# A mixture-of-experts stage on one core: twelve expert weights fetched ahead in place of nine, four token gathers before the combine weights, and two VectorE blocks cut into pieces

## The reference

```python
logits = xf @ gate_w.T                     # 1024 tokens, 32 experts
w, idx = jax.lax.top_k(logits, 2)
w = jax.nn.softmax(w, axis=-1)
combine = zeros((T, 32)).at[arange(T)[:, None], idx].add(w)
def body(acc, params):
    W, b, c = params                       # W 512 x 512, b 512, c this expert's column of combine
    return (acc + c[:, None] * (xf @ W.T + b), None)
out, _ = jax.lax.scan(body, zeros_like(xf), (expert_w, expert_b, combine.T))
x = x + tanh(g_ffn[1]) * out
```

## Time and profile before

| | us |
|---|---|
| median of 3 runs (lowest, highest) | 904.82 (903.89, 906.77) |
| the profiled execution | 904.44 |
| its span, first to last instruction | 902.6 |
| PE busy in the span | 830.1 |
| DVE busy | 656.1 |
| POOL busy | 424.7 |
| ACT busy | 397.6 |

### The profile page before, as it was taken

The page is one execution under the profiler, slowest core; times in us unless marked ns, Lnnn a source line. Parts: engine busy times, 40 slices in busy tenths (PEclk is TensorE's granted clock), DMA queues, the critical chain, the costliest instruction groups (busy, mean ns, idle before and its releaser), DMA issues. The chain is left out here.

```text
span 902.6 us, 13118 instructions
## 1 busy us (share of the span) xinstructions
PE 830.1 (92%) x4337; PEld 698.7 (77%) x4337; DVE 656.1 (73%) x1300; ACT 397.6 (44%) x1010; POOL 424.7 (47%) x386
## 2 busy tenths in 40 slices
PE   5889999999999999999999999978989897989980
PEld 4778888888888888888888888766877686877860
DVE  3788888867778867778876788774481765999975
ACT  4644244334335324324424334333224535978970
POOL 5489658336347525436634625302010257665730
PEclk9999999999999999999999999999999968999995
DMA  8401102001201101101300210007000846999717
GB/s 330 163 1 52 66 1 102 16 1 47 71 1 58 58 0 46 70 1 46 116 0 0 82 58 1 0 1 298 1 12 1 307 167 209 359 338 327 309 37 280
DMA packets 23641, 91.13 MB, mean 101 GB/s; under 512 B 6576, under 2 KB 7088, under 8 KB 15776
## 3 DMA queue, kind: packets, MB, share of 16 engines
q1 hardware_dynamic: 17440, 81.00, 24.4%
q0 software_dynamic: 6144, 9.46, 3.0%
HBM read 86.23 MB, written 14.68 MB: 112 GB/s over the span
## 5 line engine op out<-in xcount | busy, mean ns | idle before, releaser
L478 ACT ACTIVATE probs<-bank,negmax 128x128 f32<-128x128 f32 x256 | 90.7, 366 | 135.8 <-DVE negmax L605 135.8
L370 POOL TENSOR_TENSOR qT<-straight,turned 128x512 f32<-128x512 f32 x64 | 83.1, 1299 | 141.6 <-DVE turned L594 141.4
L594 DVE TENSOR_TENSOR turned<-bank,sinT 64x512 f32<-64x512 f32 x160 | 110.1, 688 | 2.2
L129 PE MATMUL bank<-wo_hi,oT_hi 128*128 128x512 f32 x256 | 100.5, 392 | 6.2 <-DVE oT_lo L618 6.2
L129 PE MATMUL bank<-xT_hi,wq_hi 128*128 128x512 f32 x256 | 104.4, 408 | 2.0 <-DVE xT_lo L105 2.0
L131 PE MATMUL bank<-xT_hi,wq_lo 128*128 128x512 f32 x256 | 100.2, 391 | 0.0
L131 PE MATMUL bank<-wo_hi,oT_lo 128*128 128x512 f32 x256 | 99.9, 390 | 0.0
L130 PE MATMUL bank<-wo_lo,oT_hi 128*128 128x512 f32 x256 | 99.7, 389 | 0.0
L130 PE MATMUL bank<-xT_lo,wq_hi 128*128 128x512 f32 x256 | 99.6, 389 | 0.0
L485 ACT ACTIVATE pT_hi<-bank 128x512 fp32r<-128x512 f32 x64 | 38.3, 599 | 128.4 <-PE bank L763 128.3
L592 DVE TENSOR_TENSOR straight<-bank,cosT 128x512 f32<-128x512 f32 x80 | 55.3, 691 | 40.5 <-PE bank L131 36.6
(11 more groups left out here) (229 smaller groups left out, 2094.2 us busy)
## 6 DMA issues: line engine op xcount, KB each, us to landing
ring<-in_ew SPq DMA_DIRECT2D x28, 1024.0 KB, 7.6
raw_big<-in_wq SPq DMA_DIRECT2D x8, 1024.0 KB, 4.8
raw_big<-in_wo SPq DMA_DIRECT2D x8, 1024.0 KB, 4.8
early_w<-in_ew SPq DMA_DIRECT2D x8, 1024.0 KB, 7.6
ring<-picked SPq DMA_DIRECT2D x8, 512.0 KB, 7.3
raw_k<-in_wk SPq DMA_DIRECT2D x8, 256.0 KB, 5.1
ctx_raw<-in_ctxT SPq DMA_DIRECT2D x4, 512.0 KB, 6.0
raw_v<-in_wv SPq DMA_DIRECT2D x8, 256.0 KB, 4.9
```

The source lines that it names most:

```text
L129: nc.tensor.matmul(out_, hi, r_hi, start=start, stop=False)
L370: nc.gpsimd.tensor_tensor(dst, straight[:, k, :], turned[:, k, :], ALU.add).then_inc(rope_sum, 1)
L478: ex = nc.scalar.activation(probs[:, u % 2, h, :], bank_scores[u % 2][:, h * S:(h + 1) * S], ACT.Exp, bias=negmax[:, u % UNITS, h:h + 1], ...
L594: last = nc.vector.tensor_tensor(turned[dst, k, :], bank[src, :], sinT[src, tok], ALU.mult)
```

## The change

1. The ring has 11 buffers that are used again, and one more (`at_far`, expert 11) that is used once, so 12 weights are fetched ahead. The two new buffers lie over the upper halves of `xT_hi` and `xT_lo`; turned tokens now use 4 tiles, the lower halves. Expert 11's weight is issued beside experts 0 and 1; experts 9 and 10 are issued with experts 2 to 6, ahead of the `xn_rows` writes. Weights 12 to 22 wait for slot k - 12, later ones for slot k - 11. `at_place` moves from `xT_lo` to the second half of `cT_lo`.
2. POOL issues `take(0)` to `take(3)` ahead of `combine_weights`.
3. COMB is 3 instead of 2: the transposes, bias matmuls and `add_bias` stand in slots 3 to 10 instead of 2 to 9.
4. `far_slots` is cut into five pieces, after slots 3 to 7. `owners` is cut into three, after slots 16 to 18, and its 16 comparisons are one operation of 512 elements. `far_places` waits until expert 11's weight has been split.
5. Semaphores are merged: the loads of context, gate weights, numbers and pair codes share `g_tables` and are all waited for at 64; `r_chosen` is counted in `r_coded`.

```diff
-        RING = 9
-        COMB = 2
+        RING = 11
+        AHEAD = RING + 1
+        TURNED = 4
+        COMB = 3
...
-        at_place = xT_lo[:, 0:2, :].rearrange("p c (j n) -> p (c j) n", n=P)
...
...
-        w_in = [sem(f"w_in{k}") for k in range(RING)]
+                over("xT_hi", "ring9", [P, KC, T])[:, :, T // 2:], over("xT_lo", "ring10", [P, KC, T])[:, :, T // 2:]]
+        w_in = [sem(f"w_in{k}") for k in range(AHEAD)]
...
+        at_far = kept("at_far", [P, NB * TOP, P], F32R)
+        ring.append(over("at_far", "ring11", [P, KC, E])[:, :, :])
...
         def turned_hi(k):
-            return xT_hi[:, :, (k % TAKEN) * P:(k % TAKEN + 1) * P]
+            return xT_hi[:, :, (k % TURNED) * P:(k % TURNED + 1) * P]
...
+        def at_place(t, k):
+            j = TOP * t + k
+            return cT_lo[:, j // 4, T // 2 + (j % 4) * P:T // 2 + (j % 4 + 1) * P]
...
+        def buffer_of(k):
+            return k if k < AHEAD else (k - AHEAD) % RING
+        def last_user(k):
+            return k - AHEAD if k < AHEAD + RING else k - RING
...
-                for k in range(EARLY):
+                for k in (*range(EARLY), RING):
                     sp.dma_start(ring[k], a["ew"][k]).then_inc(w_in[k], 16)
...
                 sp.wait_ge(g_smm, 2)
-                for k in range(EARLY, RING - 2):
+                for k in (*range(EARLY, RING - 4), RING - 2, RING - 1):
                     sp.dma_start(ring[k], a["ew"][k]).then_inc(w_in[k], 16)
                 keep_rows(TILES)
                 sp.wait_ge(g_omm, NB)
-                for k in range(RING - 2, RING):
+                for k in range(RING - 4, RING - 2):
                     sp.dma_start(ring[k], a["ew"][k]).then_inc(w_in[k], 16)
                 def weights(k, expert):
-                    after(sp, w_lo_s, 2 * (k - RING + 1))
+                    sp.wait_ge(w_lo_s, 2 * (last_user(k) + 1))
...
+        FIRST_TAKES = 4
...
-                take(0)
-                take(1)
+                for k in range(FIRST_TAKES):
+                    take(k)
                 combine_weights()
-                for k in range(2, TAKEN):
+                for k in range(FIRST_TAKES, TAKEN):
                     take(k)
...
                 def turned_upper(k):
                     act.wait_ge(t_turned, k + 1)
-                    after(act, e_mm, k - TAKEN + 1)
+                    after(act, e_mm, k - TURNED + 1)
...
                 def far_places(half):
                     pairs = slice(half * NB, half * NB + NB)
+                    dve.wait_ge(w_lo_s, 2 * AHEAD)
...
-                def owners():
-                    for j in range(16):
-                        last = nc.vector.tensor_scalar(passed[:, j, :], summed_to, float(j), None, ALU.is_le)
-                    step(last)
+                def owners(piece):
                     ready()
-                    step(nc.vector.tensor_reduce(owner[:, :], passed[:, :, :], AX.X, ALU.add))
-                    ready()
...
+                    if piece == 0:
+                        step(nc.vector.tensor_tensor(passed[:, :, :], summed_to.unsqueeze(1).broadcast_to([P, 16, NX]),
+                                                     numbers[:, 0:16].unsqueeze(2).broadcast_to([P, 16, NX]), ALU.is_le))
+                    elif piece == 1:
+                        step(nc.vector.tensor_reduce(owner[:, :], passed[:, :, :], AX.X, ALU.add))
...
                     if COMB <= k < COMB + NB:
                         add_bias(k - COMB)
-                    if k == 10:
-                        far_slots()
+                    if 3 <= k < 8:
+                        far_slots(k - 3)
                     if k in (11, 12):
                         far_places(k - 11)
...
-                    if k == 16:
-                        owners()
+                    if k in (16, 17, 18):
+                        owners(k - 16)
```

More of the change, by code:

```diff
@@ L925, in program @@
         f_turned, f_hi, f_lo, f_mm, f_sum, f_added = (sem(f"f_{n}") for n in ("turned", "hi", "lo", "mm", "sum", "added"))
-        g_bias, g_ctx, g_gate = (sem(f"g_in_{n}") for n in ("bias", "ctx", "gate"))
+        g_bias, g_tables = (sem(f"g_in_{n}") for n in ("bias", "tables"))
         (g_whi, g_wlo, g_mm, g_kept, g_smm, g_max, g_nb, g_exp, g_inv, g_turned, g_pkept, g_omm, g_added) = (
@@ L1032, in given @@
                         sp.wait_ge(y_out[lane], 16 * len(range(lane, slots, LANES)))
-                for k in range(RING, NX):
+                for k in range(AHEAD, NX):
                     weights(k, k)
@@ L1205, in expert_upper @@
                     rows = slice(2 * half, 2 * half + 2)
-                    nc.scalar.activation(expert_hi(k)[:, rows, :], ring[k % RING][:, rows, :], ACT.Copy).then_inc(w_hi_s, 1)
+                    nc.scalar.activation(expert_hi(k)[:, rows, :], ring[buffer_of(k)][:, rows, :], ACT.Copy).then_inc(w_hi_s, 1)
                 def keep_result(k):
@@ L1445, in far_starts, with far_slots @@
                     step(nc.vector.tensor_tensor(first_far[:, :], summed_to, last_full_i[:, :], ALU.subtract))
-                def far_slots():
+                def far_slots(piece):
                     pairs = [P, NB * TOP, NX]
                     ready()
-                    step(nc.vector.tensor_tensor(far_weighted[:, :, :], onehot[:, :, :, :].bitcast(F32).rearrange("p t k e -> p (t k) e"),
-                                                 first_far[:, :].unsqueeze(1).broadcast_to(pairs), ALU.mult))
-                    ready()
-                    step(nc.vector.tensor_reduce(far_slot[:, :], far_weighted[:, :, :], AX.X, ALU.add))
-                    ready()
-                    step(nc.vector.tensor_tensor(far_slot[:, :], far_slot[:, :], full[:, :], ALU.add))
-                    ready()
-                    step(nc.vector.scalar_tensor_tensor(far_slot[:, :], full[:, :], 0.0, far_slot[:, :], ALU.is_gt, ALU.mult))
-                    ready()
-                    step(nc.vector.tensor_tensor(in_far[:, :, :], numbers[:, 1:17].unsqueeze(1).broadcast_to([P, NB * TOP, 16]),
-                                                 far_slot[:, :].unsqueeze(2).broadcast_to([P, NB * TOP, 16]), ALU.is_equal))
-                    ready()
-                    nc.vector.tensor_tensor(far_code[:, :, :], in_far[:, :, :],
-                                            pair_codes[:, :, :].rearrange("p t k -> p (t k)").unsqueeze(2).broadcast_to([P, NB * TOP, 16]),
-                                            ALU.mult).then_inc(far_built, 1)
@@ new lines, in far_slots @@
+                    if piece == 0:
+                        step(nc.vector.tensor_tensor(far_weighted[:, :, :], onehot[:, :, :, :].bitcast(F32).rearrange("p t k e -> p (t k) e"),
+                                                     first_far[:, :].unsqueeze(1).broadcast_to(pairs), ALU.mult))
+                    elif piece == 1:
+                        step(nc.vector.tensor_reduce(far_slot[:, :], far_weighted[:, :, :], AX.X, ALU.add))
+                    elif piece == 2:
+                        step(nc.vector.tensor_tensor(far_slot[:, :], far_slot[:, :], full[:, :], ALU.add))
+                        ready()
+                        step(nc.vector.scalar_tensor_tensor(far_slot[:, :], full[:, :], 0.0, far_slot[:, :], ALU.is_gt, ALU.mult))
+                    elif piece == 3:
+                        step(nc.vector.tensor_tensor(in_far[:, :, :], numbers[:, 1:17].unsqueeze(1).broadcast_to([P, NB * TOP, 16]),
+                                                     far_slot[:, :].unsqueeze(2).broadcast_to([P, NB * TOP, 16]), ALU.is_equal))
+                    else:
+                        nc.vector.tensor_tensor(far_code[:, :, :], in_far[:, :, :],
+                                                pair_codes[:, :, :].rearrange("p t k -> p (t k)").unsqueeze(2).broadcast_to([P, NB * TOP, 16]),
+                                                ALU.mult).then_inc(far_built, 1)
@@ L1500, in _ @@
                 softmax_scale(0)
-                dve.wait_ge(m_in, 32)
+                dve.wait_ge(g_tables, 64)
                 attended(0)
```

72 lines of the change are left out of this document (39 added, 33 removed).

## The result

The changed kernel takes 899.47 us (median of 6 runs, 898.27 to 901.29) against 904.13 of the kernel before on the same chip (6 runs). The profiled execution took 898.27 (span 896.4).

The account below looks back on a forecast made before the run. PE's time plus its waits bound the kernel, with DVE the bound from slot 3 to 14. 7.3 + 1.7 - 1.2 = 7.8 us off 904.44 gives 896.6 us, range 894.5 to 901.5.

Parts of the forecast that it names:

- likeliest case: Whole kernel: 895 to 899 us, at 896.6, with a chance of 0.65.
- the scatters take more back: Rival: gathers at 1.93 us each make the first scatter cost 4.9 us at result 4; 900.3 us, chance 0.20.
- The gathers: Slots 1 and 2: gathers 2 and 3 issued earlier end PE's 5.6 us wait; result 2 comes 8.0 us earlier.
- The rival that moved the wait to slot 4: Combine work stretches to 9 us, slot 4's tokens land 4.5 us late, the clock slows; 902.3 us, chance 0.10.
- The scatter: Copy of result 4 waits for give(0) to land at 762.3; costs 1.2 us, ends 0.3 and 4.9.
- Gathers beside a busy DVE: POOL's five gathers could each wait for a 1.2 us split, 6 us in all by the skill; sum near 902.
- The far pieces: DVE, bias slots: cutting `far_slots` up gains nothing by itself while DVE is saturated; bounds 0.3 us either way.
- The slower rival: PE's clock falls in DVE-bound slots 4 to 14, 1.85 us lost a slot, up to 915 us; chance 0.05.
- The owners: Block that cost 2.21 us at slot 18 costs about 0.5 in pieces; gain 1.7 us, bounds 1.3 to 2.2.
- Twelve weights ahead: Weight prefetch: no slot waited for a weight, so deeper prefetch gains 0; bounds 0 and 2 us for delayed gathers.
- the prediction's own sign of being wrong: PE waiting over 2 us for slot 4's tokens, first gathers later than 736.5, or half clock between slots 4 and 14.
- 7.3: DVE up to slot 14: its split starts at 794.8 instead of 802.08, 7.3 us gained.

Follow-up runs that it names:

- e1: The changed kernel, but POOL issues takes 4 and 5, then give(k) ahead of take(k + 6): 896.82 us, ratio 0.9916.
- e2: The changed kernel with six result lanes instead of four, POOL's order unchanged: 894.58 us, ratio 0.9902.
- e4: The changed kernel, but only gathers 0 and 1 ahead of the combine weights: 902.07 us, ratio 0.9974.
- e3: The kernel before with only gathers 0 to 3 ahead of the combine weights and COMB 3: 903.49 us, ratio 0.9995.
- e8: As e1, but `far_slots` whole after slot 10, owners still in pieces: 898.05 us, ratio 0.9945.
- e10: The changed kernel with the ring of nine, buffers and early load order of the kernel before: 904.61 us, ratio 1.0011.
- e7: As e1, with the ring of nine, buffers and early load order of the kernel before: 900.36 us, ratio 0.9966.

## Why the prediction was right or wrong

**Right in direction and range.** 899.47 lies inside 894.5 to 901.5, but outside the likeliest case (895 to 899) and in that of the rival "the scatters take more back" (900.3). The sum was 7.8 us; it came to 4.7. That rival had the right wait and only in part the right reason: it wanted the first scatter issued 3.7 us later than before, and it was 1.5; the rest came from the clock. So the range was kept partly by luck: it had been widened for slow gathers, and about half of what filled it is a loss by the clock, for which this wait had no term.

**The gathers.** Forecast 8.0 us at result 2, measured 8.09 by result 2 and 8.33 by result 3. Slots 1 to 3 run at 3.27 with clock 1.00, and takes 2 and 3 cost 1.02 and 1.00. The tokens of slot 4 were on time. The prediction did not ask for those of slot 5, which were 0.75 us late; e1 and e2 show a wait there of 0.26 and 0.83. The rival that moved the wait to slot 4 is out: `combine_weights` took 5.9 us from its first instruction (740.41) to the end of its last (746.28), where that rival wanted 9.

**The scatter is the step that failed.** Its place was right: the copy of result 4. On the clock its times look right as well (give(0) forecast at 755.2, measured at 755.49; landing forecast at 762.3, measured 762.87), but that is luck, since this execution reached result 0 1.24 us earlier. Counted from the copy of result 0, give(0) is 1.5 us later than before (10.71 against 9.19 us): takes 4 to 8 cost 2.10, 1.35, 1.14, 1.43 and 1.52, between the two ends of 1.00 and 1.93 on average. The landing is 1.8 us later than forecast (18.09 against 16.28). Forecast was that DVE loses 1.2 us; with the landing 1.8 later that is 3.0, and DVE idled 2.94 ahead of weight 6. That path was understood and its input too small.

What the prediction did not have is the 1.87 us that DVE idled afterwards. PE does not read only what DVE makes: its bias matmul waits for `combT`, a copy that stands on ACT behind the waiting one, and multiply(6) for ACT and DVE. In the idle time of 1.19 and 1.74 us the clock went down, for the whole of multiply(6): its matmuls start 0.43 us apart, at 1.00 they start 0.23 apart, so 12 of them lose 2.4 us, of which DVE felt up to 1.9. Together 4.8 us in place of 1.2. e1 and e2 take the wait away and recover 4.8 and 4.9 us; that sum is shown, its division into wait and clock is read from one trace. *TensorE: Matmul & The Clock Gate* of the Trainium skill, "Part 1: The HAM clock gate", says that an idle PE drops to half clock. The trace agrees: 0.50 in the window from 768.

**Gathers beside a busy DVE.** The five gathers together took 7.54 us, 2.5 more than at 1.00. *SBUF — State Buffer* of the Trainium skill, "Who interferes with whom", would have up to 6 us for them, as the prediction worked out; the trace has less than half of it. DVE was busy 2.4 to 2.8 of 3 us in these windows. In e4, where it was busy 0.5 to 1.7 of 3, six gathers take 0.99 or 1.00 each.

**The far pieces.** "Cutting `far_slots` up gains nothing by itself" holds in e4, which has the pieces but no scatter wait: against the kernel before, slots 4 to 11 take 1.76 us more (29.88 against 28.12) and slots 12 to 14 take 2.07 less, so 0.3, the bound. It does not hold beside the scatter wait. In the changed kernel slots 12 to 14 are 2.11 us shorter and the pieces cost little where they went: the second stood where ACT waited for the scatter, the third beside the slow multiply(6). And it leaves out the clock, which a block can bring down (e3, e8) where it did not in the kernel before: about 1.3 us in e8's trace, of a difference of 4.5 to e1 that the medians show only in part. The prediction had the clock as a rival with the opposite sign, the pieces as the danger; in the changed kernel it was back at 0.96 from 772 to 776 and at 1.00 from 776 to 780, beside the last two pieces.

**The owners.** Forecast 1.7, measured 1.70 at slots 18 and 19, with operations of 0.68 us (0.73 and 0.69 forecast). In e3, which keeps the block, slot 18 takes 5.53.

**Twelve weights ahead.** Forecast 0, "as nothing there waits". By e10 it is 2.1 us of stage in the changed kernel, by e7 4.6 with earlier scatters. In the kernel before the landings were as slow (8.7 us, the median of the scatters from 828 to 858; up to 9.7) and nobody waited but for the gather of slot 2. The reading, argued from this and not tried by itself: slots that come earlier by 3 to 8 us have spent the slack that hid slow landings.

**The slower rival** (clock falling in the DVE-bound slots through their short gaps) did not occur: the window from 792 has the clock at 1.00, and the slots 7 to 11 at 3.58 on average. But the prediction's own sign of being wrong, half clock between slots 4 and 14, did, in slot 6 and by the scatter wait; and e7 shows that short gaps can be a danger.

By the prediction's own ledger: up to slot 14 it had 6.1 us (7.3 less 1.2) and got 3.15; the owners 1.7 and 1.70; the rest 0 and 0.06.

## What to carry to other kernels

When a wait goes, ask which buffer is reused next and what frees it: list that transfer's issue on its queue, its landing, and everything behind the copy on the waiting engine, not only the busiest engine's queue. A cost counted as nothing because nothing waits has to be looked at again after every gain upstream, since the slack was part of the old schedule. A block of work on a saturated engine makes TensorE idle in one length, after which its clock may fall; but cutting it up saves that only, for the pieces cost their own time wherever the engine is still the bound. And a stage length from one profile should be held against the medians: for e8 and e10 the two differ by 2 to 3 us.

## What the runs showed of the hardware

An indirect DMA's landing changes with what else is under way, and not with the rate alone (the gathers of e7 and e10 from 785 to 792 took 9.9 and 10.2 us at about the traffic at which e1's took 6.0). The scatters issued from 828 to 858 land 3.9 us (median) after issue in the changed kernel, where the last weight is issued at 833.6, and 9.8 in e10, where weights are issued up to 841.6 and the stretch from 825 moves 262 GB/s. A gather's instruction on POOL took 0.99 or 1.00 us beside a DVE busy 0.5 to 1.7 of 3 us (e4), and 1.14 to 2.10 beside one busy 2.4 to 2.8 of 3 (the changed kernel). PE's clock fell to its lower level after 2.66 us of idleness in one piece (e3, e8), after 1.19 and 1.74 us close together (the changed kernel), and after waits of 0.44, 0.73 and 0.97 us within 9 us (e7). It held 1.00 after 2.12 us in one piece in the kernel before.
